# Layer 0's experts for twelve of sixteen token tiles: from every expert for every token to blocks of chosen rows

## The reference, cut to what matters

```python
x = layernorm(x + attention(x))                       # 16 heads, causal
# layer 0 experts: 32 experts of width 96, 6 chosen per token, one shared expert of width 192
scores = sigmoid(x @ gate_w); w, i = top_k(scores, 6); w = w / w.sum()
routed = sum over the 6 chosen e of w_e * (silu(x @ wg[e]) * (x @ wu[e])) @ wd[e]
x = layernorm(x + routed + (silu(x @ sg) * (x @ su)) @ sd)
x = layernorm(x + state_space(x))                     # projection, convolution, 8 heads of decays
x = layernorm(x + experts_1(x))                       # 16 experts of width 176, 4 chosen, one shared of width 352
```

## Time and profile before

| | us |
|---|---|
| median of 3 runs | 1666.55 (1663.94 to 1666.93) |
| span of the profiled execution | 1664.1 |
| PE busy in it | 1607.4 (97%) |
| DVE, ACT, POOL busy | 1131.1, 764.6, 628.7 |
| silu of the first step starts, of the last step | 613.81, 1647.43 |

### The profile page before, as it was taken

The page is one execution under the profiler, slowest core; times in us unless marked ns, Lnnn a source line. Parts: engine busy times, 40 slices in busy tenths (PEclk is TensorE's granted clock), DMA queues, the critical chain, the costliest instruction groups (busy, mean ns, idle before and its releaser), DMA issues.

```text
span 1664.1 us, 29632 instructions
## 1 busy us (share of the span) xinstructions
PE 1607.4 (97%) x9944; PEld 1403.7 (84%) x9944; DVE 1131.1 (68%) x2877; ACT 764.6 (46%) x1889; POOL 628.7 (38%) x379
## 2 busy tenths in 40 slices
PE   7999999999999979999999999999999999999997
PEld 6988888898888868888888888888888888888886
DVE  5878878787887765556467568748784867753533
ACT  5666656666665543434433443325333533323221
POOL 2322223232222004323377335841575147533242
PEclk9999999999999999999999999999999999999999
DMA  6444335343443016666676556655655466555563
GB/s 212 159 140 143 141 118 180 132 158 139 142 141 137 1 59 205 191 196 205 199 225 188 184 176 209 194 187 165 207 189 175 146 206 197 178 175 172 195 206 107
DMA packets 101241, 277.75 MB, mean 167 GB/s; under 512 B 13488, under 2 KB 17584, under 8 KB 100112
## 3 DMA queue, kind: packets, MB, share of 16 engines
q1 hardware_dynamic: 101136, 276.39, 51.6%
HBM read 229.18 MB, written 46.63 MB: 166 GB/s over the span
## 4 chain that ended last, share of the span: by engine, by line
PE 60%; issue 14%; DVE 13%; POOL 6%; ACT 4%; DMA 1%; SPq 1%; POOLq 0%; DVEq 0%; ACTq 0%
PE psum L352 54%; POOL act_sb L578 4%; PE psum L1324 2%; DVE s_sb L1019 1%; PE psum L1335 1%; PE psum L1514 1%; POOL mix L600 1%; ACT p_sb L701 1%; PE psum L1314 1%; ACT kT_hi L660 1%; DVE s_sb L1017 1%; DVE kT_lo L913 1%; DVE pT_lo L1034 1%; DVE x L934 1%; DVE p_sb L1027 1%
## 5 line engine op out<-in xcount | busy, mean ns | idle before, releaser
L352 PE MATMUL psum<-xT_hi,gu_w 128*128 128x512 f32 x1616 | 550.3, 401 | 4.2 <-DVE act_sb L1082 4.0
L578 POOL TENSOR_TENSOR act_sb<-act_sb,comb 128x512 f32<-128x512 f32 x184 | 311.1, 1691 | 614.8 <-DVE act_sb L1082 614.6
L1082 DVE TENSOR_TENSOR act_sb<-psum,gated 128x512 f32<-128x512 f32 x204 | 140.7, 690 | 378.9 <-PE psum L352 372.6
L742 ACT ACTIVATE gated<-psum 128x512 f32<-128x512 f32 x204 | 122.2, 599 | 600.3 <-PE psum L352 597.8
L352 PEld LDWEIGHTS psum<-xT_hi,gu_w 128*128 128x128 f32 x1616 | 304.2, 188 | 78.0 <-DVE act_sb L1082 5.6
L352 PE MATMUL psum<-xT_lo,gu_w 128*128 128x512 f32 x808 | 319.6, 395 | 0.0
L352 PEld LDWEIGHTS psum<-d_w,act_hi 128*128 128x128 f32 x1632 | 221.5, 188 | 19.7 <-issue 2.1
L544 POOL TENSOR_TENSOR split_stage<-raw_stage,split_stage 128x768 fp32r<-128x768 f32 x56 | 103.1, 1840 | 354.2 <-ACT split_stage L650 354.2
L352 PE MATMUL psum<-d_w,act_hi 128*128 128x256 f32 x1632 | 227.7, 282 | 0.4 <-ACT act_hi L750 0.4
L352 PEld LDWEIGHTS psum<-xT_lo,gu_w 128*128 128x128 f32 x808 | 152.2, 188 | 28.8
L1088 DVE TENSOR_TENSOR act_lo<-act_sb,act_hi 128x512 fp32r<-128x512 f32 x204 | 148.8, 729 | 2.1 <-ACT act_hi L750 1.8
(11 more groups left out here) (203 smaller groups left out, 3473.6 us busy)
## 6 DMA issues: line engine op xcount, KB each, us to landing
gu_w<-w_split SPq DMA_DIRECT2D x204, 512.0 KB, 3.6
d_w<-w_split SPq DMA_DIRECT2D x204, 256.0 KB, 3.8
w_split<-split_stage SPq DMA_DIRECT2D x56, 768.0 KB, 3.9
raw_stage<-w_all SPq DMA_DIRECT2D x56, 384.0 KB, 4.3
decay_all<-decay_dram SPq DMA_DIRECT2D x32, 384.0 KB, 5.3
in_w<-w_split SPq DMA_DIRECT2D x40, 256.0 KB, 4.1
aw_raw<-attn_w SPq DMA_DIRECT2D x8, 1024.0 KB, 6.3
comb<-l_comb_dram SPq DMA_DIRECT2D x128, 64.0 KB, 3.1
```

Source lines behind the costliest of these rows:

```text
L352: last = nc.tensor.matmul(out_ap, w, m, start=start and n == 0, stop=stop and n == len(pairs) - 1, **kw)
L578: pool.tensor_tensor(act_sb[:, s % 2, :], act_sb[:, s % 2, :], comb[:, comb_block(s) % 2, :], ALU.mult).then_inc(comb_done, 1)
L742: act.activation(gated[to, s % 2, :], psum[0:to.stop - to.start, G_BANK, :], ACT.Silu).then_inc(gated_ready, 1)
L1082: dve.tensor_tensor(act_sb[r, s % 2, :], psum[r, G_BANK if packed(s) else U_BANK, :], gated[r, s % 2, :], ALU.mult).then_inc(t_ready, 1)
```

## The change

Quad 0 goes through layer 0 as before (steps 0 to 25). Quads 1 to 3 keep only their two shared steps each. Their experts are computed on chosen rows alone:

- The layer norm of quads 1 and 2 moves into the last attention group (`norm and i in (12, 16)` and the step behind each), that of quad 3 to step 2. The choice is made in steps 0 to 13 (`choice_logits`, `choose`, `rank`, `rows_placed`, `table`): every chosen pair of token and expert gets a row in a table `xs` in DRAM, in a region of its expert.
- `xs` is written with zeros during the attention by 42 DMAs of 1.31 MB (`zero`).
- POOL copies each token's row to its six places (`scatter`): 36 units, each of two indirect DMAs of 128 rows of 1 KB, one unit per tick, and each waits until the one before has landed. The unit of ticks is the new list `TICKS`: 26 dense steps and 2 that drain them, 12 pauses, 103 blocks, and then the other 106 steps. Scatters stand in ticks 4 to 39.
- A block is 128 rows of one expert (`BLOCKS` = 103, the most that can be needed): rows and weights are loaded (131 and 328 KB), turned (`block_turn`, 2 transposes of 128x128), multiplied in plain float32 (`block_gate_up`, 4 matmuls with 96-column weights and 128 columns; `block_down`, 1 of 256 columns), with silu, product and two copies on ACT and DVE, and stored (131 KB, two blocks in one DMA).
- Behind the blocks come the six shared steps of quads 1 to 3 and the 100 steps of layer 1. Beside them POOL gathers the results (`gather`, 36 units of two indirect DMAs, ticks in `GATHERED`), and DVE adds them with their weights three ticks later (`combine_rows`, two multiply-adds of 128x256 each).
- `FRONT` is replaced by `MARKS`, which spreads the slots o of each pair over ticks. Pair 0's first slots lie in the pauses, its slots 9 to 51 beside the blocks. Those of pairs 1 to 3 lie beside layer 1 of the quad before: slots 0 to 43 in 13 ticks for pair 1 and in 19 for pairs 2 and 3 (44 steps before), and slots 44 to 51 in 2 ticks each.

```diff
+Tick = namedtuple("Tick", "gate high down block")
+BREAK = first_step(L0, 1)
+PAUSES = 12
+
+
+def dense_ticks(a, b):
+    at = lambda s: s if a <= s < b else None
+    return [Tick(at(s), at(s - 1), at(s - LAG), None) for s in range(a, b + LAG)]
+
+
+TICKS = dense_ticks(0, BREAK) + [Tick(None, None, None, None)] * PAUSES + [Tick(None, None, None, n) for n in range(BLOCKS)] \
+    + dense_ticks(BREAK, STEPS)
+B0 = BREAK + LAG + PAUSES
+K0 = B0 + BLOCKS
+
+
+def tick_of(s):
+    return s if s < BREAK else K0 + s - BREAK
+
...
+CHOICE = {1: 0, 2: 3, 3: 6}
+COUNTED = CHOICE[3] + 4
+WEIGHED = {1: 14, 2: 17, 3: 20}
+
+PAIRS_OF = QUAD * TOP // 2
+SCATTERED = 4
+UNITS_IN = 4
+GATHERED = [K0 + u for u in range(20)] + [K0 + 24 + u for u in range(4)] + [K0 + 29 + u for u in range(8)] + [K0 + 44 + u for u in range(4)]
+COMBINED = 3
+
+
+NORM = -6
+MARKS = (((NORM, 28), (0, 33), (4, 37), (8, 39), (9, B0 + 1), (52, B0 + 92)),
+         ((NORM, K0 + 15), (-3, K0 + 17), (0, K0 + 18), (44, K0 + 31), (52, K0 + 33)),
+         ((NORM, K0 + 34), (0, K0 + 37), (44, K0 + 56), (52, K0 + 58)),
+         ((NORM, K0 + 59), (0, K0 + 62), (44, K0 + 81), (52, K0 + 83)))
+SLOTS_AT = {}
+for _p in range(PAIRS):
+    for (_v, _n), (_w, _m) in zip(MARKS[_p], MARKS[_p][1:]):
+        for _s in range(_v, _w):
+            SLOTS_AT.setdefault(_n + (_s - _v) * (_m - _n) // (_w - _v), []).append((_p, _s))
+
...
+            def zero(n):
+                by_part = xs.rearrange("(n p r) d -> n p (r d)", p=P, r=ZERO_ROWS // P)
+                dst = by_part[n] if isinstance(n, int) else by_part[bass.ds(n, 1)].rearrange("a p w -> p (a w)")
+                sp.dma_start(dst.rearrange("p (a w) -> p a w", w=BANK), zeros[:].to_broadcast([P, ZERO_ROWS // P * D // BANK, BANK])) \
+                    .then_inc(xs_zeroed, 16)
+
             def splits(g):
                 for k in range(SPLITS):
+                    if k < ZEROED:
+                        zero(ZEROED * g + k)
...
+            def weights_load(n):
+                row = first_row_of(n)
+                if n == 0:
+                    sp.wait_ge(down_done, BREAK)
+                wait(sp, b_down_done, n - BW_RING + 1)
+                sp.dma_start(block_w(n), l0_w[bass.ds(region_of(row), 1)].rearrange("a p w -> p (a w)")).then_inc(w_loaded[n % BW_RING], 16)
+
+            def rows_load(n):
+                row = first_row_of(n)
+                if n == 0:
+                    for q in ROUTED_QUADS:
+                        sp.wait_ge(scattered[q], 16 * QUAD * TOP)
+                wait(sp, xb_turned, n - XB_RING + 1)
+                sp.dma_start(xb[:, n % XB_RING, :], xs[bass.ds(row, BLOCK)]).then_inc(tokens_loaded[n % XB_RING], 16)
+
+            def block_store(n):
+                i, pair = n % 2, n // 2
+                if i == 0 and n < BLOCKS - 1:
+                    return
+                a = n - i
+                sp.wait_ge(b_copied, n + 1)
+                sp.dma_start(os[a * BLOCK:(n + 1) * BLOCK].rearrange("(i p) d -> p i d", p=P),
...
+            for i, t in enumerate(TICKS):
+                s = t.gate
+                if t.block is not None:
+                    n = t.block
+                    if n + XB_RING < BLOCKS:
+                        rows_load(n + XB_RING)
+                    if n + BW_RING - 1 < BLOCKS:
+                        weights_load(n + BW_RING - 1)
+                    if n >= 1:
+                        block_store(n - 1)
+                if i == K0 - 1:
...
+            def scatter(u):
+
+                q, v = ROUTED_QUADS[u // PAIRS_OF], u % PAIRS_OF
+                if u == 0:
+                    pool.wait_ge(xs_zeroed, 16 * ZEROED * (GROUPS - 1))
+                else:
+                    pool.wait_ge(scattered[ROUTED_QUADS[(u - 1) // PAIRS_OF]], 32 * ((u - 1) % PAIRS_OF + 1))
+                if v == 0:
+                    pool.wait_ge(placed, ROUTED_QUADS.index(q) + 1)
+                tile, ks = unit_rows(u)
+                for k in ks:
+                    pool.indirect_dma_start(xs, bass.IndirectOffsetOnAxis(ap=row_of[:, tile, k:k + 1], axis=0), x[:, FIRST_TILE + tile, :], None) \
+                        .then_inc(scattered[q], 16)
...
+            def gather(u):
+                if u == 0:
+                    blocks_stored(pool)
+                    pool.wait_ge(weighed, len(ROUTED_QUADS))
+                else:
+                    pool.wait_ge(og_loaded[(u - 1) % UNITS_IN], 32 * ((u - 1) // UNITS_IN + 1))
+                wait(pool, combined, u - UNITS_IN + 1)
+                tile, ks = unit_rows(u)
+                for j, k in enumerate(ks):
+                    pool.indirect_dma_start(og[:, u % UNITS_IN, j, :], None, os, bass.IndirectOffsetOnAxis(ap=back_of[:, tile, k:k + 1], axis=0)) \
+                        .then_inc(og_loaded[u % UNITS_IN], 16)
...
+                    if norm and i in (12, 16):
+                        q = i // 4 - 2
+                        ln_stats(q, o_added, (GROUPS - 1) * 2 * PAIRS + 2 * q + 2)
+                        ln_root(q)
+                    if norm and i in (13, 17):
+                        ln_rows(0, i // 4 - 2)
...
+            def combine_rows(u):
+
+                tile, ks = unit_rows(u)
+                to = x[:, FIRST_TILE + tile, :]
+                dve.wait_ge(og_loaded[u % UNITS_IN], 32 * (u // UNITS_IN + 1))
+                for j, k in enumerate(ks):
+                    ins = dve.scalar_tensor_tensor(to, og[:, u % UNITS_IN, j, :], mix_of[:, tile, k:k + 1], to, ALU.mult, ALU.add)
+                    if j == 0:
+                        chained(ins)
+                ins.then_inc(combined, 1)
+                dve.wait_ge(combined, u + 1)
+
+            def block_act(n):
+                h = slice(0, WIDTH)
+                dve.wait_ge(b_gated_ready, n + 1)
+                wait(dve, b_down_done, n - 1)
+                dve.tensor_tensor(b_act[h, n % 2, :], psum[h, gu_bank(n), P:2 * P], b_gated[h, n % 2, :], ALU.mult).then_inc(bt_ready, 1)
...
+            def choice_logits(q):
+
...
+                for i in range(QUAD):
+                    pairs = []
+                    for c in range(DC):
+                        t, w = slice((QUAD * q + i) * P, (QUAD * q + i + 1) * P), slice(c * SLOT, (c + 1) * SLOT)
+                        pairs += passes(xT_hi[:, c, t], xT_lo[:, c, t], hi[:, w], lo[:, w])
+                    last = chain(psum[:, choice_bank(q), i * SLOT:(i + 1) * SLOT], pairs)
...
+            def block_turn(n):
+                pe.wait_ge(tokens_loaded[n % XB_RING], 16 * (n // XB_RING) + 32)
+                wait(pe, xbT_ready, n)
+                for c in range(DC):
+                    last = pe.transpose(psum[:, TURN_BANK, c * BLOCK:(c + 1) * BLOCK], xb[:, n % XB_RING, c * P:(c + 1) * P], ident[:])
+                last.then_inc(xb_turned, 1)
+
+            def block_gate_up(n):
+                pe.wait_ge(xbT_ready, n + 1)
+                pe.wait_ge(w_loaded[n % BW_RING], w_landed(n % BW_RING, n, BREAK))
+                wait(pe, bt_ready, n - 1)
+                w, h = block_w(n), slice(0, WIDTH)
+                for i in range(2):
+                    last = chain(psum[h, gu_bank(n), i * P:(i + 1) * P],
+                                 [(w[:, c * UP + i * WIDTH:c * UP + (i + 1) * WIDTH], xbT[:, n % 2, c, :]) for c in range(DC)])
+                last.then_inc(gu_ready, 1)
+
+            def block_down(n):
+                h = slice(0, WIDTH)
+                pe.wait_ge(bt_ready, n + 1)
+                wait(pe, b_copied, n)
+                pe.matmul(psum[:, DOWN_BANK, 0:D], b_act[h, n % 2, :], block_w(n)[h, DC * UP:DC * UP + D], start=True, stop=True).then_inc(b_down_done, 1)
...
+            for i, t in enumerate(TICKS):
+                if t.block == 0:
+                    pe.wait_ge(gated_ready, BREAK)
+                    pe.wait_ge(t_ready, BREAK)
+                    pe.wait_ge(y_added, 2)
+                    block_turn(0)
+                    block_turn(1)
+                    block_gate_up(0)
+                if t.block is not None:
+                    n = t.block
+                    if n + 2 < BLOCKS:
+                        block_turn(n + 2)
+                    if n + 1 < BLOCKS:
+                        block_gate_up(n + 1)
+                    block_down(n)
```

635 lines of the change are left out of this document (467 added, 168 removed).

## The result

The changed kernel took **1865.75 us** (median of 4, 1865.69 to 1869.86) against 1665.24 of the kernel before beside it: a ratio of 1.121, with a 95% interval of 1.119 to 1.122. It is 12% slower, where 1646 was forecast, with a range up to 1705.

The account below looks back on a forecast made before the run. PE, busy for 97% of the span, was taken to set the pace. Terms of -304.6 + 4 + 7 + 3 + 45 + 168 + 15 + 4 + 36 + 2 = -20.6 gave a 1643.5 us span, 1646 as median; range 1590 to 1705.

Parts of the forecast that it names:

- The removed steps: Dense steps fall from 204 to 132, each 4.23 us of PE: -304.6 us.
- The blocks: 103 blocks of chosen rows at 1.63 us each, 1.54 of it PE's work: +168 us; interruptions by pair 0 add 15.
- rival D: A block costs PE 2.1 us through form changes or late rows: +49, 1695 us; chance 0.06.
- The two norms: Two layer norms moved into the attention's end, hidden or not: 0 to 13 us, taken as +7.
- the choice: Choice and its table beside the first dense steps, with more small matmuls on PE: +4 us (3 to 5).
- The scatters' unit: One issue and one landing, 3.7 us; 14 units back to back before the blocks make a gap costing +45 us.
- Scatters beside dense steps: 22 units between POOL's combines in ticks 4 to 25 fit barely: +3 us (0 to 15).
- Gathers: Gathers on POOL beside the rest of the work behind the blocks: +2 us (0 to 15).
- Pairs 1 to 3: State-space slots in fewer ticks: half of POOL's lag, 18, plus tails of 6 a pair, 18: +36 us (10 to 85).
- Rival A: POOL and DVE become the bound in pairs 1 to 3, late mixes stopping PE: 85 for 36, 1695 us; chance 0.20.
- Rival C: Everything is covered: lags vanish in buffers, scatters in dense steps and gathers cost nothing: 1591 us; chance 0.22.
- Rival B: Indirect DMAs' issues on POOL slow by 1.8 beside DVE, in gap, dense ticks and gathers: 1708 us; chance 0.10.

Follow-up runs that it names:

- y1: Changed kernel with two units of scatters allowed in flight, using two semaphores per quad: 1830.1 us.
- v1: Changed kernel with only `MARKS` altered, setting choice, norms' rows and turn, and slots 11 to 32 of pairs 2 and 3 in other ticks: 1804.76 us.
- v2: v1 plus POOL's combine moved behind the slots and two units of scatters in flight: 1734.94 us.

## Why the prediction was wrong, point by point

**Right.** The removed steps: the last 20 run at 4.23 as before. The blocks: alone they stand 1.53 apart (37 of the 102 distances are just that), where 1.54 was put together from short rows, and 103 of them with pair 0's slots took 217.4 against 214. Four silus in a row:

```profile
832.94 0.27 ACT L1117 ACTIVATE b_gated<-psum 96x128 f32<-96x128 f32 x1 [1.32 <-PE psum L489]
834.41 0.27 ACT L1117 ACTIVATE b_gated<-psum 96x128 f32<-96x128 f32 x1 [0.66 <-PE psum L489]
835.94 0.27 ACT L1117 ACTIVATE b_gated<-psum 96x128 f32<-96x128 f32 x1 [0.43 <-PE psum L489]
838.90 0.27 ACT L1117 ACTIVATE b_gated<-psum 96x128 f32<-96x128 f32 x1 [0.49 <-PE psum L489]
```

The 3.0 before the last are a piece of pair 0's work. No form change costs 0.19 a block, so rival D is out with its 2.1. The clock is 1.00 there. The two norms cost 8.4 for 7; the choice 5 for 4.

The 214 was right partly by luck. The forecast took 1.63 for a block because of the DMA engines, and 15 for waits for DVE and ACT. PE was busy for 193.1, which is 103 x 1.53 and 35 for pair 0, and idle for 24.3. Of that 19.7, in 17 waits, were for a block's rows to be loaded, the late rows that D had named, and only some 4 for DVE and ACT.

**The scatters' unit was right by luck, their number in the gap was not right.** 3.96 for 3.7; but the parts were one issue of 0.33 and a landing of 3.3, and are two issues of 0.97 with 0.30 between and a landing of 1.7. And POOL runs behind PE: at the silu of step 25 (754.09) there were 17 units to go (15 of them behind the last combine, where the section on the change has 14), and two of them started 8.3 and 5.3 us behind the one before, not 4.0. "14 x 3.7" should have been 17 x 4.0 and some 5 of stalls. Before the longer stall, from 767.3 to 774.2, the DMA engines were busy for 97%; that this made the landing late was not tested. PE's own work in the gap ran at a clock of 0.66, which I had called news; so of 78.8 us, not 45 but 64 were lost. The page of the Trainium skill cited above ("DMA: Bandwidth & Descriptors", section "Anatomy of one DMA — SWDGE (gpsimd) path") would have made a unit 2.6 to 2.7. The trace disagrees for units that wait for each other, since each adds two issues of 1.27 on POOL, and the measurement decides.

**Scatters beside dense steps**: +3 forecast, 13.5 measured, inside the range of 0 to 15. "It fits barely" counted POOL's issues, and those do fit (y1). What it left out is the wait for a landing in front of the next combine.

**Gathers**: +2 beside the rest and some 2 us each in the sum for the heads; measured 53. I counted POOL's time for the issues, of which there is enough, and neither the wait for the landing before, which stands in front of a combine, nor the place between a combine and a mix.

**Pairs 1 to 3, the step that failed.** "POOL is 14 behind; by the same count 15 for pair 2 and 7 for pair 3 ... half, 18", with tails of 6 a pair: 36, bounded at 85. From step 26 on the miss is 181. The working compared sums of durations per engine over six ticks, a throughput, and took the larger one for the time. That is right where each engine can run ahead of the others. Here the chain goes round through all four within one tick, so its length is the sum over the engines: 16.6 us, where POOL's share alone was 57.6 / 6 = 9.6 in the prediction. I had written down that "PE's `products` stand behind the mixes in its own order", and had even listed mixes, mix_low and products one slot apart, but never asked how many of them share a tick. Rival A had the place right, "each late mix stops PE, and a stopped PE delays the next combine", and its price wrong by the same error: it took the lags in full and not the loop. It did come out on rival A's side, though at 1866 and not A's 1695. Rival C, in which all is covered, is out with its 1591. Of the prediction's signs of being wrong the last one was met: PE waits in pairs 1 to 3 for 154.5 us, over the 60 named. And POOL was not "near 100%" there but busy for 260.5 of 622.6, 42%, and for 58.0 of the 101.9 us with pair 1's heads: too much work for POOL was the wrong picture.

**Rival B**: a gather's issue beside a scan took 2.27 us at 1228.09, where it takes 0.97 alone in the rows of the gap. That an issue of POOL is slower while DVE is at work fits the mechanism that the Trainium skill names ("SBUF — State Buffer", section "SBUF: two separate sides"); no run tests it. The mean of the 72 gathers' issues is 1088 ns, so such a slow one is rare and cannot carry the result. In the gap no issue was slowed so: all of the last 28 took 0.97.

**The miss, shared out.** Of 220: gap 19 and dense steps 12 (y1 takes 40 off both, in the traces, by another way of waiting); restart and blocks 8; the first norms 1; behind the blocks 181, of which the gathers are 53 (forecast as 2 and a part of the lags; 13 of them ahead of pair 1), and waits for a producer in the same tick at least 61 (v1, by slots alone) to 95 (v2 against y1, with the combine moved). The edits overlap, so these do not add to an exact whole, and in v2 the pairs still hold 78 us of idle time. Some 40 of them are in pair 1's stretch (181.1 long, PE busy for 140.6), where 44 slots must go into 13 ticks and could not be set apart; the others are in pairs 2 and 3, and the slow clock comes on top. What ends each of these waits was not followed further. That no order of the slots would make the idea pay was not shown; v2 is 70 us away from it.

## What to carry to other kernels

When work that was dealt out one piece per step is pressed into fewer steps, do not add up each engine's time; write down the chain from a producer to its consumer and count how many of its links fall into one step: a consumer in its producer's step puts the chain between them in the open, on every engine that it passes. Ask the same of a wait for a DMA: an issue that waits for the landing before it holds up everything behind it in its engine's order. Before an expensive edit try the cheap one: dealing the same slots out anew was worth 61 us here and changed no instruction. Two edits that each break a loop may close another one together, so measure the pair too.

## What was new of the hardware

An indirect DMA of 128 rows of 1 KB costs POOL 0.97 us with 0.30 between two, and POOL waits another 1.7 from the second issue's end for the landing. Beside one DVE scan an issue took 2.27. After PE's wait of 7.87 us the granted clock was 0.50 from 1236.34 to 1239.46, with a matmul of 512 columns taking 0.43 in place of 0.23, and 1.00 from 1240.06 on, while in the blocks, where it was idle for 24 of 217 us in pieces of up to 2.1, the clock stayed at 1.00.
